# Pixel attention: the maxima issued in two waves of two heads around the values product, other jobs ahead of it, and PSUM banks handed out by expected release

## The chip, the core and the metric

The kernel is one program on one core of a Trainium2 chip. Its time is the device time of that core in microseconds (us). TensorE is PE in the rows, VectorE DVE, ScalarE ACT, GpSimd POOL and SyncE SP; PEld is TensorE's weight load.

## The reference

An input of 8 images (256 channels, 32x32 pixels, so N = 1024 pixels) goes through four layers: a pixel attention with 32 latent channels followed by an attention on 128 concepts (L0), a class map with gates (L1), a group norm with eight-head pixel attention (L2), and a per-token attention over heads (L3). What the change touches is the pixel attention of L0 and L2:

```python
xn = ((xg - mean) * jax.lax.rsqrt(var + EPS)).reshape(B, C, T)
qkv = jnp.einsum('oc,bct->bot', w_qkv, xn) + b_qkv[None, :, None]
q, k, v = (qkv[:, :ch], qkv[:, ch:2 * ch], qkv[:, 2 * ch:])
weight = jnp.einsum('bct,bcs->bts', q * scale, k * scale)
weight = jax.nn.softmax(weight.astype(jnp.float32), axis=-1).astype(weight.dtype)
a = jnp.einsum('bts,bcs->bct', weight, v)
h = jnp.einsum('oc,bct->bot', w_proj, h) + b_proj[None, :, None]
return (x2 + h).reshape(B, C, H, W)
```

## The kernel before, in words

**Windows and steps.** Pixel attention runs in 18 windows. A window holds four heads (or, in the two windows of L0, four images of 32 channels) and has 16 steps: 8 tiles of 128 keys for the first half of 512 queries, then the same for the second. Windows 0 and 1 are L0; windows 2 to 17 are L2, an even and an odd one for each of the 8 images, called an iteration below.

**A step** on PE, in this order: `scores` writes the scores of the four heads into four PSUM banks (four passes of four matmuls, one a head: high parts, two products with the low parts, and the row maximum subtracted by a product with `NMR`). Then `values` multiplies the exponentials of the step before with V into the bank AV. Then come the step's jobs from the table that `window_jobs` makes. ACT takes the four exponentials of a step (`PR`), POOL adds up six of eight tiles of them (`ACC`), and DVE reads what the jobs leave in PSUM.

**The jobs.** `max` finds the row maxima that the half to come needs: a matmul of 128 queries by 512 keys for each of the four heads (`max_scores`), and a reduction by DVE for each (`row_max`). A half needs 8 such jobs; they stand in its first seven steps, two in step 1. `negate` and `flip` at step 7 turn the maxima into `NMR`. `qk` is a product that makes a half of q or k of the next window (`qk_product`; DVE splits it into `HI` and `LO` in `split_qk`), `v` two tiles of V (`v_product`), `post` a quarter of the output projection and residual, `sums` the softmax denominator (it needs POOL's last addition of the half before), `spread` its inverse spread out, `stats` and `gn` the group norm of the next image.

**PSUM.** Seven banks (four of `S4`, two of `RB`, and `SUM`; S, RB and SUM in the rows) form a ring. `Ring.place` gives them out in turn, in the order in which PE fills them: four for scores, four for a `max` job, one for most others. All engines count the same order. PE waits in `fill` until the last reader of a bank is done: ACT for scores (`exp_done`), DVE for the rest (`ring_free`). PE issues in order, so a wait there holds everything behind it. L3 follows after window 17 and has no ring but one bank.

Of the kernel before, what the change touches and what calls it, by code (L numbers as in the profile page):

```python
# [66 lines left out]
class Ring:  # L67


    def __init__(self):  # L70
        self.at, self.slots = 0, tuple(range(SLOTS))

    def place(self):
        self.at += 1
        return self.slots[(self.at - 1) % len(self.slots)]

    def skip(self, n):
        self.at += n

    def align(self, to=0):  # L80
        while self.at % SLOTS != to:
            self.at += 1

    def only(self, slot):
        self.at, self.slots = 0, (slot,)


def places(job, single):

    if job[0] == "v":  # L90
        return 2 if single else 1
    return {"max": 4, "stats": 0, "negate": 0, "reread": 0, "concepts": 4, "softmax": 0, "turn": 4,
            "classes": 2, "norms": 2, "pool": 0, "regate": 0, "write": 4}.get(job[0], 1)
# [9 lines left out]
QK_ORDER = ((1, 0), (1, 1), (0, 0), (0, 1))  # L103


def maxima(half):

    return [("max", half, t, keys) for t in range(TILES_HALF) for keys in range(2)]


def window_jobs(post=False, nxt=True, gn=False, ahead=0, trail=True, single=False):
# [4 lines left out]
    jobs = [[] for _ in range(STEPS)]  # L116
    for half in range(2):
        first = MT * half
        if half == 0 or nxt:
            for n, tile in enumerate(maxima(1 - half)):  # L120
                jobs[first + (n if n <= SUM_AT else n - 1)].append(tile)
            jobs[first + MT - 1] += [("negate", 1 - half), ("flip", 1 - half)]
        if half == 1 or trail:
            jobs[first + SUM_AT].insert(1, ("sums",))
            jobs[first + SPREAD_AT].append(("spread", half - 1))
    if nxt:
        for step, job in zip((1, 2, 3, MT + (3 if post or gn or single else 7)), QK_ORDER):
            jobs[step].append(("qk",) + job)
        parts = (6, MT + 1) if single else (7, MT + 1, MT + 1, MT + 2) if gn else (4, 6, 7, MT + 2)
        for n, step in enumerate(parts):  # L130
            jobs[step].append(("v", n))
    if post:
        for step, job in zip((4, 6, MT + 4, MT + 7), ((0, 0), (1, 0), (0, 1), (1, 1))):
            jobs[step].append(("post",) + job)
    if ahead:
# [3 lines left out]
        jobs[first + 2].append(("gn", 0, ahead))  # L139
    if gn:  # L140
        jobs[MT + 4].append(("gn", 1, 1))
    return jobs
# [15 lines left out]
START = [("v", 0)] + maxima(0)[:4] + [("v", 1)] + maxima(0)[4:] + [("negate", 0), ("flip", 0), ("weights",)]  # L158


def after_jobs():

    jobs = window_jobs(nxt=False)
    jobs[SPREAD_AT].remove(("spread", -1))
    jobs[3].append(("spread", -1))
    for step, stage in zip(AFTER_AT, AFTER):
        jobs[step].append(stage)
# [3 lines left out]
def first_jobs():  # L171
# [6 lines left out]
            ("norms",): [("v", n) for n in range(4)]}  # L178
    for stage, n in ((("pool",), 3), (("hidden",), 2), (("gates",), 2), (("regate",), 1)):
# [7 lines left out]
def program(nc, x, w_l0, w_o, w_o_t, concepts, concepts_t, gammas, conv_w, conv_wt, conv_b, lin1_t, lin2_t,  # L187
# [8 lines left out]
    with ctx:  # L196
# [160 lines left out]
        stage_ready = sem("stage_ready")  # L357
# [198 lines left out]
        def _(pe):  # L556
            ring = Ring()
            drained, exped, kept = Tally(), Tally(), Tally()
            held, flipped = {}, {}
# [20 lines left out]
            def qk_l0(g, which, half):  # L580
# [7 lines left out]

            def v_l0(g, part):

                qk_l0(g, 2, part)
# [49 lines left out]
            def values(u, par, s):  # L641
# [4 lines left out]
                if half == 0 and (u < 2 and mt == 0 or u > 1 and mt % 2 == 0):  # L646

                    wait(pe, v_ready, 2 * (u + 1) if u < 2 else 4 * u - 3 + mt // 2)
# [22 lines left out]
            def v_product(u, part, batch, unit):  # L671
# [3 lines left out]
                for m in range(2):  # L675
                    mt = 2 * part + m
# [5 lines left out]
            def qk_product(which, half, batch, unit):  # L682
# [7 lines left out]
                last.then_inc(ring_full, 1)  # L690

# [1074 lines left out]
```

## Time and profile before

| | us |
|---|---|
| median of 3 runs | 1922.83 (1917.22 to 1924.45) |
| profiled execution | 1920.26 |
| its span, first to last instruction | 1918.5 |
| PE busy | 1702.5 (89%) |
| DVE busy | 1374.5 (72%) |
| POOL busy | 1357.7 (71%) |
| ACT busy | 787.1 (41%) |

In the rows a line number is that of the code above. A matmul's end is modelled and matmuls overlap, so a busy PE can still be waiting; where PE loses time is read from the starts of its instructions, one behind the other. Four matmuls of four heads that work on 32 rows each run side by side ("32*128"), and so do the four of `values`, which have 32 columns each ("128*32").

### The profile page before, as it was taken

Reading aid. Unit: us, or ns where it says so; the run is one execution under the profiler, and the core shown is the slowest. Engines: PE = TensorE matmul, PEld = TensorE weight load, DVE = VectorE, ACT = ScalarE, POOL = GpSimd, SP = SyncE. Lnnn points to the kernel's source line nnn. Section 1 sums busy time; section 2 is a strip of 40 time slices with the busy share of each in tenths; the row PEclk is TensorE's granted clock in tenths of the full one; section 3 lists DMA queues with packets and bytes.
Section 4 is the critical chain, followed back from the end, with each engine's and each line's share of the span. In section 5 each row is a group of like instructions: output and inputs, shape, how many; then the busy total and the mean of one; then the engine's idle time right before and its main releaser. Section 6 shows DMA issues by size and latency. Waiting matters only on the chain.

```text
span 1918.5 us, 37187 instructions
## 1 busy us (share of the span) xinstructions
PE 1702.5 (89%) x15160; PEld 773.6 (40%) x15160; DVE 1374.5 (72%) x2153; ACT 787.1 (41%) x1546; POOL 1357.7 (71%) x581
## 2 busy tenths in 40 slices
PE   5897765799999999999999999999997678889974
PEld 2332222344344444344344344444442345555541
DVE  5677567887777877767867877777771158878875
ACT  0352401155455555455455455455555233333320
POOL 0573600088788887887888878878789059989996
PEclk8898887799999999999999999999998889999986
DMA  5000030220001001001001010010010211222211
GB/s 189 1 2 1 2 129 0 84 77 23 2 2 67 2 2 67 2 9 60 2 24 45 2 59 11 1 67 2 2 45 1 89 29 55 88 77 75 74 51 47
DMA packets 48432, 75.11 MB, mean 39 GB/s; under 512 B 30804, under 2 KB 31110, under 8 KB 48262
## 3 DMA queue, kind: packets, MB, share of 16 engines
q1 hardware_dynamic: 38758, 72.15, 10.6%
q8 instruction: 120, 1.97, 0.4%
q10 hardware_dynamic: 9504, 0.59, 0.3%
q14 instruction: 50, 0.41, 0.1%
HBM read 44.87 MB, written 25.17 MB: 37 GB/s over the span
## 4 chain that ended last, share of the span: by engine, by line
PE 77%; DVE 13%; issue 3%; ACT 2%; DMA 2%; POOL 1%; SPq 1%; POOLq 0%; DVEq 0%; ACTq 0%
PE AV L652 14%; DVE MX L1292 7%; PE S L626 6%; PE RB L895 6%; PE S L688 4%; PE S L603 3%; PE AV L908 3%; PE RB L626 3%; PE RB L944 3%; PE S L638 2%; PE RB L603 2%; PE S L630 2%; PE S L678 2%; PE RB L688 2%; PE S L634 2%
## 5 line engine op out<-in xcount | busy, mean ns | idle before, releaser
L1201 POOL TENSOR_TENSOR ACC<-ACC,PR 128x1024 f32<-128x1024 f32 x360 | 840.9, 2373 | 34.4 <-ACT PR L1034 34.4
L1034 ACT ACTIVATE PR<-S 128x512 f32<-128x512 f32 x667 | 358.6, 603 | 373.1 <-PE S L638 242.9
L1292 DVE TENSOR_REDUCE MX<-S 128x1 f32<-128x512 f32 x646 | 409.4, 681 | 124.2 <-PE RB L603 60.5
L1201 POOL TENSOR_TENSOR ACC<-PR 128x1024 f32<-128x1024 f32 x72 | 168.9, 2368 | 343.0 <-ACT PR L1034 131.6
L652 PE MATMUL AV<-PR,VT 128*32 128x512 f32 x2304 | 312.9, 616 | 3.8 <-ACT PR L1034 3.3
L1292 DVE TENSOR_REDUCE MX<-RB 128x1 f32<-128x512 f32 x336 | 218.5, 681 | 73.8 <-PE S L603 57.0
L1034 ACT ACTIVATE PR<-RB 128x512 f32<-128x512 f32 x328 | 183.7, 604 | 168.9 <-PE S L638 63.4
L626 PE MATMUL S<-HI 32*128 32x512 f32 x667 | 195.6, 493 | 6.2 <-DVE NMR L1305 2.5
L1227 POOL TENSOR_TENSOR PR<-WO,WRK 128x1792 f32<-128x1792 f32 x32 | 155.6, 4883 | 27.9 <-DMA WO<-WO 12.9
L1227 POOL TENSOR_TENSOR PR<-WO,VT 128x1792 f32<-128x1792 f32 x32 | 155.0, 4867 | 10.3 <-DMA WO<-WO 8.3
L603 PE MATMUL S<-HI 32*128 32x512 f32 x646 | 156.2, 507 | 3.4 <-ACT PR L1034 2.8
L1651 DVE TENSOR_REDUCE ENC<-PR 128x256 f32<-128x2048 f32 x64 | 145.9, 2280 | 15.7 <-issue 7.4
L630 PE MATMUL S<-LO,HI 32*128 32x512 f32 x667 | 143.1, 431 | 0.0
L1292 DVE TENSOR_REDUCE MX<-SUM 128x1 f32<-128x512 f32 x170 | 115.8, 681 | 34.4 <-PE S L603 33.7
L638 PE MATMUL S<-NMR,ONER 32*128 32x512 f32 x667 | 131.6, 397 | 0.0
L634 PE MATMUL S<-HI,LO 32*128 32x512 f32 x667 | 131.2, 397 | 0.0
L1034 ACT ACTIVATE PR<-SUM 128x512 f32<-128x512 f32 x157 | 94.8, 604 | 75.3 <-PE S L638 69.1
L626 PEld LDWEIGHTS S<-HI 32*128 32x128 f32 x667 | 78.7, 183 | 108.9 <-ACT PR L1034 39.2
L626 PE MATMUL RB<-HI 32*128 32x512 f32 x328 | 118.1, 491 | 4.0 <-ACT PR L1034 2.0
L603 PE MATMUL RB<-HI 32*128 32x512 f32 x336 | 111.5, 509 | 11.1 <-DVE MX L1292 11.1
L895 PE MATMUL RB<-X 128*32 128x256 f32 x1792 | 111.7, 390 | 10.6 <-ACT X L1099 4.2
L603 PEld LDWEIGHTS S<-HI 32*128 32x128 f32 x646 | 59.4, 186 | 140.3 <-DVE MX L1292 48.7
(357 smaller groups left out, 3250.9 us busy)
## 6 DMA issues: line engine op xcount, KB each, us to landing
X<-out_y SPq DMA_DIRECT2D x24, 1024.0 KB, 5.0
out_y<-X SPq DMA_DIRECT2D x16, 1024.0 KB, 4.9
X<-in_x SPq DMA_DIRECT2D x8, 1024.0 KB, 8.5
OHU<-out_y SPq DMA_DIRECT2D x8, 512.0 KB, 4.4
X<-out_y SPq DMA_DIRECT2D x8, 512.0 KB, 4.1
out_y<-X SPq DMA_DIRECT2D x8, 512.0 KB, 3.1
out_y<-OHU SPq DMA_DIRECT2D x8, 512.0 KB, 3.1
WO<-WO SPq DMA_DIRECT2D x128, 16.0 KB, 1.9
```

The source lines that it names most:

```text
L603: mm(bank(), HI[par][D * h:D * h + D, 0, first:first + P], HI[par][D * h:D * h + D, 1, HALF * keys:HALF * keys + HALF], start=True, stop=T ...
L626: mm(dst[h], HI[par][row, 1, keys], HI[par][row, 0, cols], start=True, stop=False, skip_group_check=True)
L630: mm(dst[h], HI[par][row, 1, keys], LO[par][row, 0, cols], start=False, stop=False, skip_group_check=True)
L634: mm(dst[h], LO[par][row, 1, keys], HI[par][row, 0, cols], start=False, stop=False, skip_group_check=True)
L638: mm(dst[h], ONER[row, :], NMR[row, half, :], start=False, stop=True, skip_group_check=True).then_inc(st_full, 1)
L652: last = mm(AV[D * h:D * h + D, :], VT[par][:, mt, D * h:D * h + D], exps(s, h // 2)[:, HALF * (h % 2):HALF * (h % 2) + HALF], start=(mt = ...
L895: last = mm(dst[D * j:D * j + D, QUARTER * (h % 2):QUARTER * (h % 2) + QUARTER], W3[:, t, C * which + D * h:C * which + D * h + D], xn3(b) ...
L1034: nc.scalar.activation(exps(s, pair)[:, HALF * one:HALF * one + HALF], RING[ring.place()], ACT.Exp, scale=1.0 if i is None else float(D) * ...
L1201: nc.gpsimd.tensor_tensor(ACC[:, pair, :], so_far, exps(s, pair), ALU.add).then_inc(pool_used, 1)
L1227: nc.gpsimd.tensor_tensor(PV[n % 2].rearrange("p (h d g) -> p h d g", h=NHEAD, d=D)[:, heads], PTK[:, st, heads, j, :].unsqueeze(2).broadc ...
L1292: nc.vector.tensor_reduce(out=MX[:, h, t, keys:keys + 1], in_=bank(), op=ALU.max, axis=AX.X).then_inc(ring_free, 1)
L1651: nc.vector.tensor_reduce(out=O3[n % 2], in_=PV[n % 2].rearrange("p (c g) -> p c g", g=NHEAD), op=ALU.add, axis=AX.X).then_inc(o_ready3, 1)
```

## The change

The ring gives each step's banks out by a plan (`Ring.begin`): a list of the banks in the order in which they are expected to come free, in which the banks of the first wave of maxima stand between those of the scores, and all others behind. The maxima of a half are now 16 jobs of two heads each, over keys 0 to 511 first and then over the rest; a step has one `max` job right behind its scores, and one or two `late` ones behind `values`. All other jobs stand between the first wave and `values`, save in steps 7 and 15, where they stay behind `values`. A v product makes four tiles in place of two. q and k of the next window are made at steps 0, 2, 8 and 10 in place of 1, 2, 3 and 11 or 15; V at steps 3 or 4, and 7. The wait on `stage_ready` becomes one on the exact split that a wave reads.

```diff
 class Ring:
     def __init__(self):
-        self.at, self.slots = 0, tuple(range(SLOTS))
+        self.free, self.step = list(range(SLOTS)), []
 
     def place(self):
-        self.at += 1
-        return self.slots[(self.at - 1) % len(self.slots)]
+        if self.step:
+            return self.step.pop(0)
+        self.free.append(self.free.pop(0))
+        return self.free[-1]
...
+    def begin(self, jobs, single):
+        held = []
+
+        def take():
+            if not self.free:
+                self.free.append(held.pop(0))
+            self.step.append(self.free.pop(0))
+            return self.step[-1]
+
+        for _ in range(H):
+            held.append(take())
+        for job in jobs:
+            for n in range(places(job, single)):
+                slot = take()
+                held.insert(2 * n + 1 if job[0] == "max" else len(held), slot)
+        self.free += held
...
-QK_ORDER = ((1, 0), (1, 1), (0, 0), (0, 1))
+QK_ORDER = ((1, 0), (0, 0), (1, 1), (0, 1))
+LATE = (1, 2, 1, 1, 2, 1, 1)
...
         if half == 0 or nxt:
-            for n, tile in enumerate(maxima(1 - half)):
-                jobs[first + (n if n <= SUM_AT else n - 1)].append(tile)
+            waves = maxima(1 - half)
+            for n, count in enumerate(LATE):
+                jobs[first + n].append(waves.pop(0))
+                late[first + n] = [("late",) + waves.pop(0)[1:] for _ in range(count)]
...
-        for step, job in zip((1, 2, 3, MT + (3 if post or gn or single else 7)), QK_ORDER):
+        for step, job in zip((1, 2, 3, MT + 3) if single else (0, 2, MT, MT + 2), QK_ORDER):
             jobs[step].append(("qk",) + job)
-        parts = (6, MT + 1) if single else (7, MT + 1, MT + 1, MT + 2) if gn else (4, 6, 7, MT + 2)
-        for n, step in enumerate(parts):
+        for n, step in enumerate((6, MT + 1) if single else (4, 7) if gn else (3, 7)):
             jobs[step].append(("v", n))
     if post:
-        for step, job in zip((4, 6, MT + 4, MT + 7), ((0, 0), (1, 0), (0, 1), (1, 1))):
+        for step, job in zip((3, 5, MT + 4, MT + 7), ((0, 0), (1, 0), (0, 1), (1, 1))):
...
-            def max_scores(u, par, half, t, keys):
-                if t == 0 and keys == 0:
-                    wait(pe, stage_ready, 2 * u + half + 1)
+            def max_scores(u, par, half, n):
+
+                keys, t, pair = n // (2 * TILES_HALF), n // 2 % TILES_HALF, n % 2
+                if n % (2 * TILES_HALF) == 0:
+
+                    wait(pe, ring_free, max(kept_qk[u, 0, half], kept_qk[u, 1, keys]))
                 first = HALF * half + P * t
-                for h in range(H):
+                for h in (2 * pair, 2 * pair + 1):
...
                 for s in range(STEPS):
+                    ring.begin(jobs[s], i is None)
                     scores(u, par, s)
-                    if s:
-                        values(u, par, s - 1)
-                    elif ("sums",) in jobs[SUM_AT]:
-                        values(u - 1, 1 - par, STEPS - 1)
-                    for job in jobs[s]:
-                        if job[0] == "spread":
+                    behind = [job for job in jobs[s] if job[0] == "late" or s % MT == MT - 1]
+                    for job in jobs[s][:len(jobs[s]) - len(behind)] + [("values",)] + behind:
+                        if job[0] == "values" and s:
+                            values(u, par, s - 1)
```

What stands on PE at steps 2 and 3 of an even window of L2, from one `values` to the next. Before (L603 is the maxima, L688 a q or k product, L626 to L638 the four passes of the scores, L652 `values`; in brackets, the semaphores waited for, `exp_done` for ACT's exponentials and `ring_free` for DVE's reads):

```order
L652 MATMUL AV<-PR,VT 32x512 [waits exp_done]
L652 MATMUL AV<-PR,VT 32x512 x3
L603 MATMUL S<-HI 128x512 [waits ring_free] x2
L603 MATMUL RB<-HI 128x512 [waits ring_free]
L603 MATMUL RB<-HI 128x512 [waits exp_done]
L688 MATMUL SUM<-X 128x512 [waits exp_done]
L688 MATMUL SUM<-X 128x512
L626 MATMUL S<-HI 128x512 [waits exp_done] x2
L626 MATMUL S<-HI 128x512 [waits ring_free] x2
L630 MATMUL S<-LO,HI 128x512 x4
L634 MATMUL S<-HI,LO 128x512 x4
L638 MATMUL S<-NMR,ONER 128x512 x4
```

After, at step 2 from the last pass of its scores on (L667 that pass, L632 the maxima, L717 the q or k product, L681 `values`, L655 the first pass of the next scores):

```order
L667 MATMUL S<-NMR,ONER 128x512 x2
L667 MATMUL RB<-NMR,ONER 128x512 x2
L632 MATMUL SUM<-HI 128x512 [waits ring_free]
L632 MATMUL S<-HI 128x512 [waits ring_free]
L717 MATMUL S<-X 128x512 [waits ring_free]
L717 MATMUL S<-X 128x512
L681 MATMUL AV<-PR,VT 32x512 [waits exp_done]
L681 MATMUL AV<-PR,VT 32x512 x3
L632 MATMUL S<-HI 128x512 [waits exp_done]
L632 MATMUL SUM<-HI 128x512 [waits ring_free]
L655 MATMUL S<-HI 128x512 [waits exp_done]
L655 MATMUL S<-HI 128x512 [waits ring_free]
```

The product went from behind the maxima to between the first wave and `values`, and the bank that it takes is now one that DVE frees where it was one that ACT frees.

At step 1 after the change, PE has two late jobs (four matmuls) between `values` and the scores of step 2, whose fourth bank DVE frees (`half_kept` is ACT's copy of the sums):

```order
L681 MATMUL AV<-PR,VT 32x512 [waits exp_done,v_ready,half_kept]
L681 MATMUL AV<-PR,VT 32x512 x3
L632 MATMUL RB<-HI 128x512 [waits exp_done]
L632 MATMUL SUM<-HI 128x512 [waits ring_free]
L632 MATMUL S<-HI 128x512 [waits exp_done]
L632 MATMUL S<-HI 128x512 [waits ring_free]
L655 MATMUL S<-HI 128x512 [waits exp_done] x2
L655 MATMUL RB<-HI 128x512 [waits half_kept]
L655 MATMUL RB<-HI 128x512 [waits ring_free]
```

The four maxima of a step, which stood together, are now two before and two or four behind `values`; the last scores bank waits for the first of the late ones.

## Rows read from the trace of the kernel before

**Rows 1.** The page, busy us and share of the span, by engine.
```profile
PE 1702.5 (89%) x15160; PEld 773.6 (40%) x15160; DVE 1374.5 (72%) x2153; ACT 787.1 (41%) x1546; POOL 1357.7 (71%) x581
```

**Rows 2.** Busy time by stretch: PE, PEld, DVE, ACT, POOL, clock, DMA.
```profile
514.80:1353.50 838.70, 828.90 (x6530) 359.53 (x6528) 638.63 (x1106) 422.59 (x817) 692.86 (x324) 0.99 0.07 24
60.00:131.30 71.30, 66.64 (x572) 25.10 (x564) 49.85 (x82) 34.19 (x68) 56.09 (x24) 0.95 0.01 1
131.30:376.40 245.10, 171.42 (x1033) 69.64 (x1032) 174.51 (x234) 54.88 (x85) 60.67 (x30) 0.80 0.08 31
```

**Rows 3.** Timeline (start, length), PE and DVE in a step without another job.
```profile
755.83 1.06 PE L652 MATMUL AV<-PR,VT 128*32 128x512 f32 x8
756.82 0.51 PE L603 MATMUL S<-HI 32*128 32x512 f32 x3
757.36 1.89 DVE L1292 TENSOR_REDUCE MX<-S 128x1 f32<-128x512 f32 x3 [2.13 <-PE RB L603]
758.05 0.55 PE L626 MATMUL S<-HI 32*128 32x512 f32 x2
759.23 0.64 PE L652 MATMUL AV<-PR,VT 128*32 128x512 f32 x4
```

**Rows 4.** The chain that ended last: start, us, what.
```profile
740.53 0.99 PE AV L652 x8
741.98 1.09 PE S L678 x8
743.07 0.42 PE S L626
744.52 0.99 PE AV L652 x8
...
758.60 0.23 PE S L630 x2
...
759.30 0.99 PE AV L652 x8
760.77 3.08 DVE MX L1292 x5
763.89 0.49 PE S L626
765.09 0.99 PE AV L652 x8
```

**Rows 5.** The same chain at steps with jobs.
```profile
726.09 1.00 PE S L662 x8
727.09 0.86 PE S L667 x8
...
728.37 1.92 PE S L688 x4
...
749.35 1.06 PE S L712 x2
...
753.57 0.30 PE S L611
...
833.83 1.99 PE S L678 x16
```

**Rows 6.** Timeline of DVE behind a q or k product, and at statistics.
```profile
735.29 0.74 DVE L1267 TENSOR_SCALAR HI<-S,X 128x512 fp32r<-128x512 f32 x1
736.06 0.75 DVE L1268 SCALAR_TENSOR_TENSOR LO<-S,X,HI 128x512 fp32r<-128x512 f32 x1
...
772.95 1.27 DVE L1326 BATCH_NORM_STATS2 BN<-X 128x6 f32<-128x512 f32 x2
```

**Rows 7.** What POOL waited for, from 514.8 to 1353.5, and one norm between additions.
```profile
L1201 POOL TENSOR_TENSOR ACC<-PR 128x1024 f32<-128x1024 f32 x48 | 112.6, 2368 | 145.4 <-PE S L667 83.0 <-PE RB L667 37.7 <-PE SUM L667 24.7
...
852.17 0.70 POOL L1172 TENSOR_TENSOR RSTD<-VE,MHALF 128x2 f32<-128x2 f32 x1
...
856.12 9.37 POOL L1201 TENSOR_TENSOR ACC<-ACC,PR 128x1024 f32<-128x1024 f32 x4
```

More of the change, by code:

```diff
@@ L99, in wait, with window_jobs @@
         eng.wait_ge(sem, value)
-QK_ORDER = ((1, 0), (1, 1), (0, 0), (0, 1))
+QK_ORDER = ((1, 0), (0, 0), (1, 1), (0, 1))
+LATE = (1, 2, 1, 1, 2, 1, 1)
 def maxima(half):
-    return [("max", half, t, keys) for t in range(TILES_HALF) for keys in range(2)]
-def window_jobs(post=False, nxt=True, gn=False, ahead=0, trail=True, single=False):
+    return [("max", half, n) for n in range(4 * TILES_HALF)]
+def window_jobs(post=False, nxt=True, gn=False, ahead=0, trail=True, single=False, side=()):
     jobs = [[] for _ in range(STEPS)]
+    late = [[] for _ in range(STEPS)]
     for half in range(2):
@@ L138, in window_jobs @@
         jobs[first + 1].append(("stats", 1, ahead))
-        jobs[first + 2].append(("gn", 0, ahead))
+        jobs[first + (2 if ahead == 2 else 3)].append(("gn", 0, ahead))
     if gn:
-        jobs[MT + 4].append(("gn", 1, 1))
-    return jobs
+        jobs[MT + 5 if ahead else MT + 3].append(("gn", 1, 1))
+    for step, stage in side:
+        jobs[step].append(stage)
+    return [job + waves for job, waves in zip(jobs, late)]
 AFTER = [("reread", 0), ("encode", 0), ("concepts", 0), ("softmax", 0), ("encode", 1), ("turn", 0), ("mix", 0),
@@ L154 @@
 AFTER_AT = (3, 3, 4, 5, 5, 6, 7, 7, 8, 9, 10, 10, 11, 12, 13, 13, 14, 15)
-START = [("v", 0)] + maxima(0)[:4] + [("v", 1)] + maxima(0)[4:] + [("negate", 0), ("flip", 0), ("weights",)]
+START = [("v", 0)] + maxima(0)[:8] + [("v", 1)] + maxima(0)[8:] + [("negate", 0), ("flip", 0), ("weights",)]
 def after_jobs():
-    jobs = window_jobs(nxt=False)
+    jobs = window_jobs(nxt=False, side=[(3, ("spread", -1))] + list(zip(AFTER_AT, AFTER)))
     jobs[SPREAD_AT].remove(("spread", -1))
-    jobs[3].append(("spread", -1))
-    for step, stage in zip(AFTER_AT, AFTER):
-        jobs[step].append(stage)
     return jobs
@@ L177, in first_jobs @@
             ("classes",): [("qk",) + job for job in QK_ORDER[2:]],
-            ("norms",): [("v", n) for n in range(4)]}
-    for stage, n in ((("pool",), 3), (("hidden",), 2), (("gates",), 2), (("regate",), 1)):
+            ("norms",): [("v", n) for n in range(2)]}
+    for stage, n in ((("pool",), 6), (("hidden",), 4), (("gates",), 4), (("regate",), 2)):
         jobs[stage] = tiles[:n]
@@ L578, in all_read, with placed_l0 @@
                 wait(pe, ring_free, drained.now())
-            def qk_l0(g, which, half):
+            def placed_l0(g, which, half):
                 dst = bank()
@@ L587, in qk_l0 @@
                 last.then_inc(ring_full, 1)
+            def qk_l0(g, which, half):
+                placed_l0(g, which, half)
+                kept_qk[g, which, half] = drained.now()
             def v_l0(g, part):
-                qk_l0(g, 2, part)
+                placed_l0(g, 2, part)
                 all_read()
@@ L674, in v_product @@
                     pe.wait_ge(wv_in, 16)
-                for m in range(2):
-                    mt = 2 * part + m
+                for m in range(4):
+                    mt = 4 * part + m
                     for t in range(CT):
@@ L690, in qk_product @@
                 last.then_inc(ring_full, 1)
+                kept_qk[u, which, half] = drained.now()
             def group_sums(k, batch):
```

71 lines of the change are left out of this document (37 added, 34 removed).

## The prediction

> **What bounds the kernel now.** The page first: PE is busy 89% of the span, DVE 72%, POOL 71% [rows 1]. The windows that repeat, 3 to 16, show it better: the six iterations from 514.8 to 1353.5 take 838.7 us, 139.8 each, and PE is busy for 828.9 of them, DVE for 638.6, POOL for 692.9 [rows 2]. DVE and POOL have room; POOL waits 145.4 us there, all of it for PE's sums [rows 7]. So a window's length is that of PE's order, with whatever PE waits for inside its "busy" time.
>
> Next the timeline of one step with no other job. From one values product to the next it takes 3.40 us (755.83 to 759.23), and it is a loop with DVE: the maxima start 0.99 behind values, DVE's first reduction 1.53 behind, its end is 2.21 behind, and there the last scores bank opens; four passes more and values starts again, 1.19 later [rows 3]. Reductions follow each other every 0.60 (five end 3.08 after the first began, [rows 4]). This gives a rule that I check on two other places. If the last bank of the scores is freed by reduction k (k = 0 the first), the interval is 2.21 + 0.60k + 1.19: for k = 1 that is 4.00, and the row says 3.99 (740.53 to 744.52); for k = 4 it is 5.80, and the chain, which runs through five reductions of DVE there, says 5.79 (759.30 to 765.09) [rows 4]. Without waits the interval would be 0.99 for values, 0.43 for the maxima and four passes of 0.23: 2.34.
>
> An interval with a q or k product is 0.99 + 0.43 + 1.91 for the product + 1.12 for the scores = 4.45 (the scores are 0.42 and three passes of 0.23), all PE: DVE reads the maxima while the product runs. That cover is what the change takes away.
>
> **What the change costs and gives, interval by interval.** The work is the same: 32 maxima a half, four q and k products and 8 V tiles a window. What moves is where PE waits. Seven banks are given out, and scores, first wave and one job need 4 + 2 + 1, all seven. So a job ahead of values takes the bank that comes free last, that of the last late reduction of the step before; the order of the changed program shows it (`ring_free` where `exp_done` stood). From values that reduction is ready, with one late job, at 2.26 + 0.60 = 2.86 (the 0.05 is from release to matmul), and with two late jobs (steps 1, 4, 9, 12) at 2.26 + 1.80 = 4.06. PE itself could start the job at 2.34. Behind a split of q or k, DVE is busy first: HI and LO take 1.52 from 0.1 behind the product [rows 6], so the late reductions start at 1.57 in place of 1.53, and I take 2.90.
>
> The jobs: a q or k product 1.91 (1.92 in the row), and a post product of the same shape as much; a whole V part takes 1.99, sums 1.86, spread 1.05, flip or group sums 0.30 [rows 5]. The interval is then the ready time plus the job. For one iteration, even and odd window, 32 intervals (named by the steps of their values products, s to s+1):
> - late wave, then sums, 0-1 and 8-9: 2.90 + 1.86 = 4.76, four times, 19.0
> - two late waves, then a q or k product, 1-2 and 9-10: 4.06 + 1.91 = 5.97, four times, 23.9; before, that interval took 4.45 plus little
> - 2-3: 4.89 (V, odd) and 4.81 (post, even), 9.7
> - 3-4: V in the even window 4.85; in the odd no job, and the first wave waits for the first late reduction, 2.26 + 0.32 = 2.6; 7.5
> - 4-5: post behind two late waves 5.97 (even); without a job the scores wait for the first late reduction and the first wave for the third, 3.8 (odd); 9.8
> - 5-6, spread: 2.86 + 1.05 = 3.9, twice, 7.8
> - 6-7 and 14-15, nothing in front of values: 2.35, four times, 9.4
> - 7-8 (flip, V, scores, first wave, q or k product): 0.99 + 0.14 + 1.99 + 1.12 + 0.15 + 1.91 = 6.3, twice, 12.6
> - 15-0: 6.3 behind a post, 5.3 without one (the scores then wait for DVE's flip), 11.6
> - 10-11: even 3.2 (group sums), odd 2.7; 5.9
> - 11-12: even, post 4.77; odd, the statistics (two of 0.64 and a little, about 1.55 on DVE [rows 6]) push the late reductions to 2.95, 3.95; 8.7
> - 12-13: even 3.8; odd, statistics and two late waves, 5.8; 13-14: 3.9 and 4.1; 17.6
>
> The sum is 143.5 against 139.8: **+3.7 us an iteration**. It is a small difference of large terms. Against the present intervals the four with products behind two waves lose 1.5 each, the other eleven with a job ahead of values lose 0.3 to 0.5 for the wait, and those with no job gain (3.40 to 2.35, 2.6 or 2.7; two of them only lose 0.4, at two late waves).
>
> Six such iterations give +22. The first, without post, and the last even window add 3 (the even window +2.3 like the others, the rest from the same rule), and window 17, which makes nothing for a next one, gains about 3, since its intervals are the jobless ones. Windows 0 and 1 (71.3 and 245.1 us, [rows 2]): in window 0 two products lose 1.5 and 0.4 and the jobless steps gain as much; window 1 is a ping-pong of PE and DVE stages whose work stays, and fewer maxima stand ahead of each stage. I take 0 for both, with 4 us either way. L3 is not touched. Where an edit costs nothing: the removed `stage_ready` is two sequencer instructions hidden in DVE's waits. POOL: twelve additions of a half must fit between two sums. POOL waits 145.4 us there over 24 halves, 6.1 a half, and where a norm stands between the additions it takes 3.95 of that (852.17 to 856.12) [rows 7]. The halves do not get shorter on average, so POOL stays covered; at some 2 us less in a half with a norm, its additions would be late next. No DMA is issued at another place but the two small ones of ACT for the inverse, and these have a whole step.
>
> So 1920.3 + 22.5 = 1943 in the profiled execution; the median before lies 2.6 above its profiled execution, within the spread of the runs, and I say **1944**.
>
> **A rule weighed.** The first matmul after a change from 32-row tiles to a 128-row product or back takes 0.42 where its like takes 0.23 [rows 4]. The Trainium skill, "TensorEngine Tiling (Array Packing)", Key Properties, says that changing the tiling mode drains TensorE. A step with a job changes mode four times before and three times after, for the late wave, the scores and the first wave stand together. By that rule 0.2 comes back in each such interval; by the rows it comes back only where PE does not wait for a bank anyway, and I count it nowhere.
>
> **Rivals.**
> *One mode change fewer is not hidden* (no change). If PE's waits for the job's bank overlap less than I say, by 0.2 in each of 15 intervals with a job, an iteration is 3.0 shorter, eight give 24 and the time is 1920. For it: the difference of 3.7 is 0.12 an interval, of the size of what I round. Against it: the rule of reductions came out to 0.01 at three places. 0.15.
>
> *The waits before jobs are covered* (faster). If the last late reduction were done when PE arrives, at 2.34, the intervals would be 4.2 with sums (four), 5.4 with a product behind two waves (four), 4.3 with others, 2.35 without: 129.5 an iteration, 10 less than before, and about 1840 in all. It decides at the place between values and a job: the late reduction must end before 2.34 behind values. A wave issued at 0.99 whose first reduction starts at 1.53 cannot. Half of it, 1890, needs DVE's reductions to be faster than 0.60. All of the faster side: 0.13.
>
> *The late reductions push more than one step* (slower still). DVE's order is first wave, job, late wave; a split ends at 1.65 and everything behind it on DVE moves, statistics above all. If each interval loses 0.1 more, 32 of them in 8 iterations add 26: 1970. 0.07 beyond.
>
> **Chances.** My forecast, slower by 0.5 to 2.5%: 0.65; no change 0.15; faster 0.13; slower beyond that 0.07. About 0.5% is what a measurement can tell from no change: faster 0.13, same 0.15, slower 0.72. The range that leaves the faster side and the far slow side out is 1913 to 1972.
>
> **What would show it.** In the changed profile: an interval from step 1 to 2 of about 6.0 and from 0 to 1 of 4.8 (before 4.6 and 6.8, when it held a product too); 2.35 at 6 to 7; PE's products (line 717) idle in front for DVE's maxima, where now they wait for nothing; iterations of 143 to 144. Wrong would be: products that start 2.35 behind values, iterations under 139, or POOL's wait for the sums gone, which would mean that the halves have become short.

## The result, and the profile after

The changed kernel takes 1950.9 us (median of 4 runs, 1948.87 to 1954.12) against 1923.64 for the kernel before (4 runs, 1917.22 to 1924.79): ratio 1.015, with a 95% interval of 1.0123 to 1.0177. It is slower, as forecast, by 27 us where 21 had been forecast. Its profiled execution took 1954.12, with a span of 1952.3.

The page of the changed kernel, busy time by engine and the shares of the chain that ended last:

```profile
PE 1682.5 (86%) x15160; PEld 774.7 (40%) x15160; DVE 1377.9 (71%) x2121; ACT 790.3 (40%) x1546; POOL 1359.0 (70%) x581
...
PE 62%; DVE 26%; issue 5%; ACT 2%; POOL 2%; DMA 2%; SPq 1%; POOLq 0%; DVEq 0%; ACTq 0%
```

The work is that of [rows 1]: each engine is busy about as long as before (PE 20 us less; its waits within a wave count in part as busy, which probably makes the difference). Yet DVE now holds 26% of the chain, and it held 13% before. Time in which PE stood behind a busy engine has become time in which it waits for one.

By stretch, as in [rows 2]: the six iterations, window 2, and windows 0 and 1:

```profile
517.00:1389.20 872.20, 820.39 (x6532) 362.42 (x6528) 639.85 (x1080) 425.19 (x816) 693.85 (x324) 0.98 0.07 23
373.50:446.30 72.80, 66.67 (x537) 29.47 (x540) 54.22 (x95) 35.43 (x69) 59.39 (x30) 0.95 0.26 98
62.00:373.50 311.50, 230.73 (x1596) 93.70 (x1588) 226.10 (x312) 88.75 (x151) 114.65 (x54) 0.85 0.07 26
```

The six iterations take 872.2 where they took 838.7: +33.5, or 145.4 each against 139.8. Windows 0 and 1 take 311.5 against 316.4 (71.3 and 245.1 in [rows 2]), 5 less. What is left adds up to another 5 more: 2.2 ahead of window 0, 5.1 in windows 2 and 3, 1.2 in window 16, and 3.1 less from window 17 on. So the loss is in the iterations.

The chain that ended last, in the even window that begins at 807, from the `values` (L681) of step 1 on. The names behind PE and DVE are the tensors written: S, RB and SUM are banks of the ring; L717 is a q or k product, L735 a post product, L742 spread, L1301 and L1302 the split:

```profile
807.61 0.86 PE AV L681 x8
808.47 0.42 PE RB L632
...
808.93 2.48 DVE MX L1324 x4
...
811.46 2.00 PE S L717 x4
...
813.49 0.76 DVE HI L1301
...
814.27 0.75 DVE LO L1302
815.02 1.20 DVE MX L1324 x2
...
816.27 1.98 PE SUM L735 x4
818.26 0.99 PE AV L681 x8
...
829.09 1.00 PE AV L681 x8
...
830.56 1.29 DVE MX L1324 x2
...
831.98 1.10 PE SUM L742 x2
833.08 1.00 PE AV L681 x8
```

This is what the forecast said PE would wait for. Behind two late waves the product starts only when DVE has done all four reductions, at 811.46. By the timeline `values` had started at 807.42, so that is 4.04 behind it (forecast 4.06), and the next `values` starts at 813.38. Behind that product DVE has the split to do before the two late reductions, and the post product starts at 816.27, 2.89 behind (forecast 2.90). In front of spread, where no split stands between, `values` started at 829.02 by the timeline and the matmul at 831.98, 2.96 behind (forecast 2.86). While one of these jobs runs, DVE has little to do; while DVE reduces the late wave, PE can issue nothing. In [rows 5] the same product stood behind the maxima and DVE's time lay under it.

The 32 intervals from `values` to `values`, worked out from their starts in the trace (windows 8 and 9 of each kernel), beside the list in the prediction:

```
steps      even: before after forecast     odd: before after forecast
0-1              3.40   4.64   4.76             3.41   4.63   4.76
1-2              6.78   5.95   5.97             6.77   5.96   5.97
2-3              4.59   4.81   4.81             4.62   4.88   4.89
3-4              4.48   4.85   4.85             4.49   2.69   2.6
4-5              4.52   5.98   5.97             3.98   3.88   3.8
5-6              3.39   3.99   3.9              3.40   3.99   3.9
6-7              5.33   2.35   2.35             4.59   2.36   2.35
7-8              3.29   6.31   6.3              3.40   6.31   6.3
8-9              3.42   4.64   4.76             3.40   4.64   4.76
9-10             6.98   5.95   5.97             5.79   5.96   5.97
10-11            4.00   3.21   3.2              3.99   2.72   2.7
11-12            4.48   4.79   4.77             3.40   3.96   3.95
12-13            4.63   3.89   3.8              4.07   6.17   5.8
13-14            3.41   3.99   3.9              5.52   5.68   4.1
14-15            3.99   2.36   2.35             4.62   2.35   2.35
15-0             4.19   6.26   6.3              4.16   5.38   5.3
```

(The first row is that of the next window's step 0 to 1.) A row does not hold the same jobs before and after, since the products and V moved to other steps: 1-2 held the sums and a product before and is shorter now, while 0-1 and 7-8 got a job and are longer. Only the sums of a column compare the kernels. Thirty of the 32 are within 0.13 of the forecast. The odd window's 12-13 and 13-14 are not: together 11.85 against 9.9. There the granted clock falls. By stretches of 2 us in the odd window that begins at 881 (columns as in [rows 2], the clock third from the end):

```profile
930.00:932.00 2.00, 0.70 (x7) 0.19 (x3) 1.82 (x5) 0.00 (x0) 2.00 (x2) 1.00 0.08 12
932.00:934.00 2.00, 1.53 (x15) 1.08 (x15) 2.00 (x4) 0.33 (x1) 2.00 (x2) 0.77 0.00 0
934.00:936.00 2.00, 2.00 (x13) 0.71 (x10) 1.93 (x8) 1.73 (x4) 2.00 (x2) 0.50 0.00 0
936.00:938.00 2.00, 2.00 (x16) 1.05 (x16) 0.42 (x2) 0.00 (x0) 2.00 (x2) 0.50 0.00 0
940.00:942.00 2.00, 2.00 (x18) 0.54 (x20) 1.34 (x3) 0.95 (x2) 1.95 (x1) 1.00 0.00 0
```

The wait in it, from the timeline of PE (in brackets, how long PE stood idle before it, and for what):

```profile
932.47 0.50 PE L655 MATMUL RB<-HI 32*128 32x512 f32 x1 [1.77 <-DVE MX L1324]
```

And the chain through it (L1358 is statistics):

```profile
930.14 1.21 DVE BN L1358 x2
...
931.72 0.70 DVE MX L1324
...
932.47 0.50 PE RB L655
...
934.97 1.86 PE AV L681 x8
...
943.01 1.00 PE AV L681 x8
```

From 930 to 932 PE has 0.70 of 2 us of work, since it waits 1.77 us for DVE, which has two statistics (1.21) ahead of the reduction that frees the next bank. The clock then goes from 1.00 to 0.50, that is from 2.4 to 1.2 GHz, and the same eight matmuls of `values` take 1.86 in place of 1.00. In the six iterations the low clock covers 10.2 us of the kernel before and 34.1 of the changed one, all of it in odd windows. The Trainium skill, "TensorE: Matmul & The Clock Gate", in its section on PSUM-queue depth-cycling, tells of a kernel whose clock falls because PE idles between groups of matmuls as it cycles through its banks; these rows agree (1.00 granted, a wait of 1.77 us, then 0.50).

The kernel before shows the same thing at the same steps, in three of its six odd windows of the iterations; here in the one that begins at 724.6:

```profile
778.00:780.00 2.00, 1.19 (x5) 0.66 (x5) 1.82 (x5) 0.42 (x1) 2.00 (x2) 1.00 0.02 4
780.00:782.00 2.00, 1.99 (x17) 1.06 (x21) 1.69 (x7) 0.66 (x2) 2.00 (x2) 0.61 0.00 0
```

The three windows with 3.4 us of low clock take 69.6 to 69.7 us, the three without 68.1 to 68.4, in the same order of work. So 3.4 us of low clock cost about 1.4 there.

### The profile page after: what moved, and what is told of

Its sections match the earlier page's. It is cut to its first block, busy times and chain, and to the rows that moved or that the text cites. A ratio compares the mean times of both kernels' runs of the same rounds, so it can differ in the third digit from the quotient of the medians.

```text
span 1952.3 us, 37066 instructions
## 1 busy us (share of the span) xinstructions
PE 1682.5 (86%) x15160; PEld 774.7 (40%) x15160; DVE 1377.9 (71%) x2121; ACT 790.3 (40%) x1546; POOL 1359.0 (70%) x581
## 3 DMA queue, kind: packets, MB, share of 16 engines
q1 hardware_dynamic: 38758, 72.15, 10.4%
## 4 chain that ended last, share of the span: by engine, by line
PE 62%; DVE 26%; issue 5%; ACT 2%; POOL 2%; DMA 2%; SPq 1%; POOLq 0%; DVEq 0%; ACTq 0%
DVE MX L1324 15%; PE AV L681 10%; PE RB L928 6%; PE S L632 3%; PE AV L941 3%; PE S L717 3%; PE RB L977 2%; PE S L707 2%; DVE HI L1301 2%; DVE LO L1302 2%; PE SUM L717 2%; PE RB L632 2%; PE RB L717 1%; PE S L655 1%; PE S L735 1%
## 5 line engine op out<-in xcount | busy, mean ns | idle before, releaser
L1068 ACT ACTIVATE PR<-S 128x512 f32<-128x512 f32 x696 | 384.8, 603 | 413.5 <-PE S L667 298.9
L681 PE MATMUL AV<-PR,VT 128*32 128x512 f32 x2304 | 314.5, 618 | 3.0 <-ACT PR L1068 3.0
L1068 ACT ACTIVATE PR<-RB 128x512 f32<-128x512 f32 x367 | 215.2, 604 | 174.7 <-PE S L667 111.3
L1324 DVE TENSOR_REDUCE MX<-RB 128x1 f32<-128x512 f32 x292 | 195.9, 681 | 65.7 <-PE SUM L632 29.8
L632 PE MATMUL S<-HI 32*128 32x512 f32 x617 | 225.8, 488 | 4.2 <-DVE MX L1324 3.5
L655 PE MATMUL S<-HI 32*128 32x512 f32 x696 | 188.9, 464 | 31.5 <-DVE MX L1324 20.7
L1324 DVE TENSOR_REDUCE MX<-SUM 128x1 f32<-128x512 f32 x243 | 165.0, 679 | 12.6 <-PE S L632 9.7
L632 PEld LDWEIGHTS S<-HI 32*128 32x128 f32 x617 | 90.7, 189 | 171.0 <-DVE MX L1324 70.9
L655 PE MATMUL RB<-HI 32*128 32x512 f32 x367 | 144.0, 467 | 14.4 <-DVE MX L1324 13.3
L663 PE MATMUL S<-HI,LO 32*128 32x512 f32 x696 | 151.9, 398 | 0.0
L667 PE MATMUL S<-NMR,ONER 32*128 32x512 f32 x696 | 151.7, 397 | 0.0
L632 PE MATMUL RB<-HI 32*128 32x512 f32 x292 | 128.4, 491 | 4.1 <-DVE MX L1324 4.0
L632 PE MATMUL SUM<-HI 32*128 32x512 f32 x243 | 116.8, 481 | 10.2 <-DVE MX L1324 9.9
L659 PE MATMUL RB<-LO,HI 32*128 32x512 f32 x367 | 125.3, 422 | 0.0
```

Of the source, the lines that this page charges most:

```text
L632: mm(bank(), HI[par][D * h:D * h + D, 0, first:first + P], HI[par][D * h:D * h + D, 1, HALF * keys:HALF * keys + HALF], start=True, stop=T ...
L655: mm(dst[h], HI[par][row, 1, keys], HI[par][row, 0, cols], start=True, stop=False, skip_group_check=True)
L659: mm(dst[h], HI[par][row, 1, keys], LO[par][row, 0, cols], start=False, stop=False, skip_group_check=True)
L663: mm(dst[h], LO[par][row, 1, keys], HI[par][row, 0, cols], start=False, stop=False, skip_group_check=True)
L667: mm(dst[h], ONER[row, :], NMR[row, half, :], start=False, stop=True, skip_group_check=True).then_inc(st_full, 1)
L681: last = mm(AV[D * h:D * h + D, :], VT[par][:, mt, D * h:D * h + D], exps(s, h // 2)[:, HALF * (h % 2):HALF * (h % 2) + HALF], start=(mt = ...
```

## The experiments

Two theories stood against each other. **The bank**: what costs is that a job ahead of `values` takes the bank of the last late reduction and so waits for DVE. **The order itself**: it is the split into two waves, the plan of the banks, or DVE's order that costs. Times are medians; ratios are against the kernel before on the same chip. Where an edit shifts the line numbers, the text ahead of the rows names them.

**Jobs last.** All jobs other than maxima behind `values` and the late wave; split, plan and product steps of the change stay.

```diff
-    return [job + waves for job, waves in zip(jobs, late)]
+    first = [[job for job in step if job[0] == "max"] for step in jobs]
+    rest = [[job for job in step if job[0] != "max"] for step in jobs]
+    return [a + waves + b for a, waves, b in zip(first, late, rest)]
...
-                    behind = [job for job in jobs[s] if job[0] == "late" or s % MT == MT - 1]
+                    behind = [job for job in jobs[s] if job[0] != "max"]
```

> The changed kernel with its two waves and its bank plan, but every job other than the maxima behind values and behind the late wave. Theory (a job ahead of values must take the seventh bank, which DVE frees last): the job no longer waits, an interval with a q or k product falls from 4.8 to 6.0 down to about 4.5 to 4.65, intervals without a job stay at 2.35 to 3.9, an iteration falls from 145.4 to about 134 us, and the kernel to about 1880 us, below the kernel before. Rival (two waves in place of one cost PE more, wherever the jobs stand): an iteration stays above 139.8 and the kernel above 1924 us.

1901.51 us, ratio 0.9904 (0.9883 to 0.9924): 49 less than the changed kernel by one edit, and less than before. The intervals 1-2 and 4-5 of even windows fall from 5.95 and 5.98 to 4.76 and 4.79. But it is 20 above what was expected: an interval with a job takes 4.70, and in each odd window the clock is low for 10.2 us, with 5.37, 5.53 and 5.37 for the intervals from 12 to 15 in window 7.

**Banks in turn.** The changed order, but `Ring.place` gives the banks out in turn, as before.

```diff
     def place(self):
-        if self.step:
-            return self.step.pop(0)
         self.free.append(self.free.pop(0))
         return self.free[-1]
```

> The changed kernel with the banks given out in turn as before, the order of the work left as changed. Theory: scores, first wave and job fill all seven banks in either way, so the job takes the bank of the last late reduction here too; the intervals with jobs stay at 4.8 and 6.0, an iteration within 1 us of 145.4, the kernel 1945 to 1960 us. Rival (the bank plan is what costs): the kernel falls back to about 1924 us.

1949.68 us, ratio 1.0145 (1.0129 to 1.0162), the changed kernel's own. In this order the plan is neither the loss nor a gain.

**Shorter reductions, after and before.** `row_max` reads 256 of the 512 columns of each bank, in the changed kernel and in the kernel before, so half of the keys are left out of the maxima.

```diff
-                    nc.vector.tensor_reduce(out=MX[:, h, t, keys:keys + 1], in_=bank(), op=ALU.max,
+                    nc.vector.tensor_reduce(out=MX[:, h, t, keys:keys + 1], in_=bank()[:, 0:HALF // 2], op=ALU.max,
```

> The changed kernel whose row maxima are reduced over 256 of the 512 columns of each bank (the other half of the keys of a bank is left out of the maximum). Theory: with reductions of about 0.42 us, 0.34 apart, a job's bank is ready at 2.34 behind values, where PE arrives by itself; an iteration falls from 145.4 to about 129 us and the kernel to about 1830 us, which is faster than the kernel before with the same cut. Rival (the order itself or changes of tiling mode cost): it falls no more than the kernel before does with this cut, some 50 us, to about 1900 us.

> The kernel before with the same cut of the reductions (half of each bank's columns left out of the maximum). Theory: an interval without a job falls only from 3.40 to about 3.15 to 3.2, where ACT's exponentials end next, those with a product stay at 4.45; an iteration falls by about 6 us and the kernel to about 1875 us, so it lies above the changed kernel with this cut. Rival: the difference of 27 us between the two kernels stays as it is.

1828.82 us (0.9522, 0.9504 to 0.954) and 1854.19 us (0.9654, 0.9627 to 0.9682). A reduction takes 0.416 where it took 0.681:

```profile
L1324 DVE TENSOR_REDUCE MX<-S 128x1 f32<-128x256 f32 x617 | 242.7, 416 | 139.5 <-PE S L632 75.7 <-PE SUM L632 36.0 <-PE RB L632 26.7
```

PE's work is the same, and still the changed kernel gives back 122 us and the kernel before 66 (from 1920.63 on that chip). With short reductions the changed order is the faster by 25. So DVE's reductions are the price of the changed order; a part of it goes through the clock, since no stretch of the six iterations is low in the changed kernel with the cut, where 34.1 us were. The kernel before fell by more than expected (1875), but not in its iterations: these fell by 36 us, 6.0 each, as expected. Another 29 lie ahead of them, 6.4 before window 0, 16.1 in windows 0 and 1, and 6.3 in windows 2 and 3, which the expectation left out.

**The late wave moved.** In odd windows the second double wave goes from step 12 to step 14, behind the statistics; once with the jobs last, once in the changed kernel alone.

```diff
+LATE_ODD = (1, 2, 1, 1, 1, 1, 2)
...
-            for n, count in enumerate(LATE):
+            for n, count in enumerate(LATE_ODD if ahead == 2 and half else LATE):
```

> As e1_jobs_last, but in the odd windows the second double wave of the second half stands at step 14 in place of 12, away from the statistics of steps 11 and 12. Theory (PE waits for DVE behind statistics and a double wave, its granted clock then falls to half and stretches the steps 13 and 14): the low-clock stretch of 10.2 us in each odd window goes away, the four intervals from step 10 to 14 fall from 19.1 to about 15.5 us, an iteration from 139.9 to about 136 and the kernel to about 1872 us. Rival (the clock falls in each odd window for another reason): the low stretch stays, and the kernel within 10 us of 1901.

> The changed kernel with nothing altered but that move of one double wave from step 12 to 14 in the odd windows. Theory: intervals 12 to 13 and 13 to 14, 5.8 to 6.2 and 5.1 to 6.3 now, fall to about 4.6 and 4.0, interval 14 to 15 rises from 2.35 to about 3.4, no low-clock stretch is left in the odd windows; the kernel falls by about 14 us to 1936. Rival: the loss is only moved, the kernel stays at 1950.

With the jobs last 1885.82 us (0.9812, 0.9785 to 0.984), the fastest kernel here that takes the maxima over all keys, and 14 above what was expected; in the changed kernel 1941.19 (1.0094, 1.0072 to 1.0117), 9.7 less than without, where 14 had been expected. In the first no stretch of the six iterations has a low clock and they take 136.2 each (817.4, from 499.6 to 1317.0, over six); in the second 3.4 us is left of 34.1, and the odd intervals 12-13 and 13-14 take 4.65 and 4.04 where they took 6.17 and 5.68, while 14-15, which has the double wave now, takes 3.39 for 2.35. The three together fall from 14.20 to 12.08 (window 9). Without the clock the prediction's terms gave 12.25 for them unmoved (5.8 + 4.1 + 2.35), so by these terms the move itself is worth little and most of the gain is the clock.

The chain of the kernel with the jobs last and the wave moved, at steps 2 to 3 of an even window (L684 `values`, L635 the maxima, L720 a q or k product, L658 the first pass):

```profile
776.91 1.00 PE AV L684 x8
777.91 0.43 PE S L635 x2
778.34 1.91 PE SUM L720 x4
780.25 0.43 PE RB L658
...
781.38 0.23 PE S L635
781.61 0.99 PE AV L684 x8
```

All PE: DVE reduces under the product. The interval is 0.99 + 0.43 + 1.91 + 0.43 + three passes and the first wave of 0.23, 4.68 (measured 4.70). In the kernel before it was 4.45 by the terms of [rows 5] (4.48 measured at 3-4): a wave of two heads takes PE as long as one of four, 0.23 or 0.43, and that is paid each step.

**The waves together where there is a job.** As the last, but a step with a job has both its waves behind `values`, to save that 0.23.

```diff
+    for n in range(STEPS):
+        if first[n] and any(job[0] not in ("stats", "gn") for job in rest[n]):
+            late[n], first[n] = [("late",) + first[n][0][1:]] + late[n], []
```

> As e5_last_moved, but the first wave stands ahead of values only in steps that have no product, sums or spread; in the others both waves stand behind values, ahead of the job. Theory: a wave of two heads that is cut off from the other by a job costs PE one pass (0.23), so intervals with a job fall from 4.70 to 4.48 and those without stay at 2.7 to 3.9; an iteration falls to about 133 us and the kernel to about 1850 us. Rival (both waves together bring back the waits of the kernel before): no faster than e5_last_moved.

1907.86 us, ratio 0.9914 (0.9894 to 0.9935). Wrong by 58: some intervals do take 4.48 to 4.52, but others wait again, 5.18 (1-2), 5.35 (4-5) and 5.69 (12-13). The rival holds: with both waves behind `values` the waits of the kernel before come back, and they cost more than 0.23.

**One wave, jobs last.** The same loop for every step of the kernel with the jobs last, `if first[n]:` alone.

> As e1_jobs_last, but in every step the first wave too stands behind values, so that the maxima are one wave again, with the changed bank plan and the changed steps of the products. Theory (the two waves are what shortens intervals without a job): these go back to 3.40, those with a product to 4.48; an iteration comes out at 139 to 141 us, the kernel at 1905 to 1925 us. Rival (the bank plan or the moved products give what e1 gained): the jobless intervals stay below 3.0.

1956.57 us, ratio 1.0172 (1.0143 to 1.0201), above what was expected: steps with two maxima take 5.2 to 5.3. The clock is low for 47.8 us of the six iterations, but for 61.4 in the first experiment, so it is not the difference. This run takes away more than its expectation says. `Ring.begin` places only the banks of `max` jobs between those of the scores, and here no `max` job is left: the list is then the turn. So with the jobs last the split and the plan together are worth 55 us by the medians, 52 by the ratios, and this run does not divide them.

**Jobs behind `values` but ahead of the late wave.** The edit of the first experiment to `behind`, with the jobs left ahead of the late ones.

> The changed kernel with all jobs behind the values product but still ahead of the late wave, so between the changed kernel (job ahead of values, 1950) and the one with jobs behind the late wave (1901). Theory A, only the wait for the job's bank costs: values hides it (the bank is ready 2.9 behind the values before, PE reaches the job only 1 us into the next interval), the intervals with a product are 4.5 to 4.8, and the time is 1900 to 1910. Theory B, the place of the split in DVE's order counts as well: DVE begins the split 2.9 behind values, ends it at 4.5, and the late reductions of the step follow only then, the first at about 5.1; where the last scores bank is one of theirs the interval is 5.1 + 1.2 = 6.3, where only the first wave needs one it is 5.4. Then the gain of no wait is lost again and the time is 1935 to 1955. I expect B.

2007.31 us, ratio 1.0456 (1.0438 to 1.0473): slower than either neighbour, and slower than expected. The chain (lines as in the changed kernel):

```profile
677.03 0.99 PE AV L681 x8
678.03 1.93 PE S L717 x4
...
679.98 0.76 DVE HI L1301
...
680.76 0.75 DVE LO L1302
681.51 0.61 DVE MX L1324
...
682.17 0.50 PE RB L632
682.67 1.00 PE AV L681 x8
```

The wait for the job's own bank is gone (the product starts 1.00 behind `values`), and yet the interval is 5.64: the product, DVE's split, and one late reduction now stand in series ahead of the next first wave. The bank theory alone gave 1900 to 1910 and falls. The cause that fits all the runs is wider: whatever PE issues, DVE's work on it and DVE's reductions must lie under PE's work, and a job issued before the late wave puts both into one chain. Only a job that stands last in its step is covered by reductions that are already on their way.

**The banks in turn, jobs last.** The turn in the fastest kernel.

> The kernel with the jobs last and the moved late wave (1886), with the banks in turn instead of the plan. In the changed kernel the plan was worth nothing, since there a job takes the last bank whatever the list. Theory: with the jobs last all seven banks are again given to scores and waves before the job, each in the order in which its reader comes, and the turn gives nearly the same banks as the plan: 1886, within 6 us. Rival: with the jobs last the list's one real step, to place the first wave's banks between those of the scores, saves a wait for the fourth scores bank in the steps without a job (2.7 against 3.4), about 0.7 in 5 of 32 intervals, and 8 iterations give 28: 1910.

1922.81 us, ratio 1.0008 (0.9997 to 1.0019). The first guess was wrong and the rival nearer, in size though not in place: the plan is worth 37 us here. The loss is in the steps with a double late wave: 1-2 takes 5.21 against 4.76, 4-5 5.33 against 4.78. Chain and timeline of such a step (L619 the maxima, L678 the job behind them):

```profile
790.65 0.44 PE S L619 x3
...
791.10 0.49 PE S L619
791.58 0.62 PE RB L678
```

```profile
789.47 1.58 ACT L1055 ACTIVATE PR<-S 128x512 f32<-128x512 f32 x3 [2.14 <-PE S L654]
```

The fourth late matmul starts 0.45 behind the others, when ACT has finished the third exponential of the same step (789.47 + 1.58 = 791.05). In turn the four late matmuls take the last free bank and those of the first three scores. By `Ring.begin` the plan gives them the free one, the first scores bank, one of the first wave that DVE has read, and the second scores bank, whose exponential ends earlier; in the kernel with the plan all four start within 0.01. The 26.8 us that the six iterations lose divide evenly: 13 in the even windows, which have no low clock with or without the plan (71.4 for 69.2), and 14 in the odd ones, where it is low for 30.7 us with the turn and never with the plan.

**Jobs ahead of `values` in the kernel before.** One part of the change alone, on the old kernel.

```diff
-    return jobs
+    return [step if s % MT == MT - 1 else [job for job in step if job[0] != "max"] + [job for job in step if job[0] == "max"]
+            for s, step in enumerate(jobs)]
...
+                    ahead = ("qk", "v", "post", "sums", "spread", "gn", "stats") if s % MT < MT - 1 else ()
+                    front = [job for job in jobs[s] if job[0] in ahead]
+                    for job in front + [("values",)] + [job for job in jobs[s] if job[0] not in ahead]:
```

> The kernel before with one part of the change alone: the jobs that are not maxima stand ahead of values (save at steps 7 and 15), the maxima in one wave of four behind it. Theory: what costs is that a job ahead of values no longer lies in the time in which DVE reduces. The last scores bank still waits for the first reduction of the step before, 2.21 behind values, so the scores end at 3.40 behind values as in a step without a job, and the job adds its whole length: a q or k product gives 3.4 + 1.9 = 5.3 where it took 4.5, a V part of 1.0 gives 4.4 where the step took 3.5 to 4. That is 0.8 to 0.9 in about 12 of 32 intervals, 10 an iteration, 80 in eight: 2000, more than the changed kernel, which has the second wave to pay part of it back. Rival: the place ahead of values costs only together with the late wave that holds its bank; then one wave with the jobs ahead is within 10 of before, 1913 to 1933.

> The kernel before with one part of the change alone, as in the run before this one (there a bank in window 1, in L0, was counted out of order between the engines; this mends it, and the windows of L2 are as they were): jobs other than maxima ahead of values, the maxima in one wave of four behind it. The trace of that run tells what to look for: behind a product, values and two full waves, DVE has the split (1.5) and up to eight reductions (0.6 each) to do, and the scores that follow wait for the fifth of them, so the interval from step 0 to 1 is 10.4. Theory: a job ahead of values brings the whole wave behind DVE's work on that job, 2130 to 2145 here, and the changed kernel's second wave is what takes most of that back; from 1923 the jobs alone cost 210 and the split and the plan give back 190. Rival: the time of the run before came from window 1, and with the bank counted right it is under 2050.

2138.59 us in the first form (1.1146, 1.1122 to 1.1170), whose window 1 takes a bank out of the order that the other engines count, and 2140.78 in the second, which does not (1.1147, 1.112 to 1.1174). The direction was right and the size far off at first (2000). The chain from step 1 to 2 of an odd window, in the second form (the expectation calls it 0 to 1; L627 the first pass, L689 a q or k product, L653 `values`):

```profile
976.44 0.76 DVE HI L1271
...
977.23 0.75 DVE LO L1272
977.98 2.40 DVE MX L1296 x4
...
980.42 1.39 PE S L627 x2
...
983.09 3.71 PE S L689 x4
986.80 1.19 PE AV L653 x8
```

The split and whole waves stand on DVE between the product and the next scores, the interval is 10.4, and the clock falls on top: the product takes 3.71 in place of 1.92, and the granted clock has a mean of 0.912. So the jobs ahead of `values` are the costly part, 218 us alone, and the rest of the change gives back 190 of them: the split, the other steps of the products, and the plan, of which the second experiment shows no gain in this order.

## Why the forecast was right, by its steps

- **The rule of reductions** held: ready 2.96 with one late wave, 2.89 behind a split, 4.04 with two (forecast 2.86, 2.90, 4.06).
- **The list of 32 intervals** gave 143.5, measured 145.4. 30 terms are within 0.13, and right in sum by 0.1 since their errors cancel: the four with sums came out 0.12 or 0.13 short, seven others 0.08 or 0.09 long.
- **The term that was mis-sized**: the odd window's 12-13 and 13-14 ("statistics and two late waves, 5.8; 13-14: 3.9 and 4.1"). They took 11.85 in place of 9.9 in window 9, 11.06 in window 7, and 11.7 in the mean of the six iterations. The prediction priced the wait and not the clock behind it; [rows 2] had 0.99 for the iterations, and the low stretches in it were never looked at. With the wave moved and the clock back, an iteration takes 143.6. The six iterations are 11.3 above the forecast's 22.2, and the profiled execution is 11 above 1943.
- **The edges** came out right in sum by luck. Windows 0 and 1 took 5 less, where 0 with 4 either way was said; 2.2 came on ahead of window 0, where nothing was said; windows 2, 3 and 16 took 6.3 more in place of 3. Window 17 took 1.1 less in place of 3, and what follows it another 2.0 less, in code that the change does not touch. Together that is 0.3 from the forecast. In the working, "+2.3 like the others" for an even window is not what the prediction's own list gives: that is 74.0 against 70.9, +3.1, and 73.97 was measured.
- **The account against the present intervals** was wrong. The prediction put the 6.8 and 4.6 of before at 0-1 and 1-2; they are those of 1-2 and 2-3. The four with products behind two waves do not "lose 1.5 each": 1-2 went from 6.78 to 5.95, 9-10 from 6.98 to 5.95 in even windows and from 5.79 to 5.96 in odd ones. The larger losses are at 0-1 and 8-9 (1.2 each), 7-8 (3.0 and 2.9), 15-0 (2.1 and 1.2), 4-5 (1.5, even) and 12-13 (2.1, odd). The total of 143.5 does not hang on it, but window 0 does: its "two products lose 1.5 and 0.4" was worked out so, and the interval 1-2 there went from 8.69 to 6.12.
- **POOL** stayed covered. Its wait for the sums grew, as it must when halves get longer, from 145.4 to 165.9:

```profile
L1235 POOL TENSOR_TENSOR ACC<-PR 128x1024 f32<-128x1024 f32 x48 | 112.5, 2365 | 165.9 <-PE S L696 100.8 <-PE RB L696 65.1
```

- **The rule on tiling modes** was counted nowhere, and the intervals with a job came out without it to 0.03 at 1-2, 2-3 and 11-12. None of its 0.2 came back there, where PE waits for a bank. The four intervals with sums are the exception: from the start of sums to that of `values` it is 1.74 (805.68 to 807.42) where 1.86 was counted, and both have the tiling "128*32", so a mode change that is gone may show there; no run separates it. As a forecast of no change the first rival ("one mode change fewer is not hidden") is out.
- **The second rival**, waits covered, would have needed the late reduction done at 2.34; the job started at 2.89 at the earliest. Covered waits come only once the jobs stand last: 1886 to 1901. The third (more than one step pushed, 1970) did not happen in the changed kernel, but it is the mechanism of the one with the jobs behind `values` and ahead of the late wave, 2007.
- **What the prediction did not see**: that the plan of the banks, worth nothing here, is worth 37 us with the jobs last (and the wave moved), and plan and split together 52 to 55 (wave not moved). If the two bases may be mixed, an estimate, the split alone has some 15 to 18 of these. The change combines what can be gains with one loss that is larger.

Open is what the split does alone, with the banks in turn; why the clock falls in some odd windows of the kernel before and not in others, with the same order of work; and how the changed kernel would do with other steps for its products. None of these was tried.

## What to carry to other kernels

Where two engines feed each other through a ring of banks, try a long job of one directly behind the work that it has just handed to the other, so that the job's own follow-up comes last too; here that was worth 49 us against the place ahead of `values`, and 106 against the one ahead of the late wave. Count for every place of a job not only the bank that it needs but what its reader has queued ahead of the next release. And take a split, an order and an allocation apart before judging them: here the order was the loss, and the allocation was worth 0 or 37 us, depending on it.

## What the runs showed of the hardware

The granted clock fell where short groups of matmuls alternate with waits for DVE: idle 0.74 us before 928.30 and 1.77 before 932.47, then 0.50 granted from 934 to 938, although PE is fully busy in that time. Most matmuls then take about twice as long: `values` 1.86 for 1.00, a product 3.71 for 1.92. In the kernel before with its jobs ahead of `values` the low clock covers 376 us of the span against 232. A wait that brings it about costs more than its length.

A reduction of half the columns takes 0.416 for 0.681. If the time grows evenly with the columns, some 0.15 of it does not depend on them; that is an estimate from two points.
